# A two-layer transformer tower on one core: normalisation moved to ScalarE, one part of the maxima moved behind the values, three pieces of weights rounded later

## The reference

```
h = W.T[x] + b + pe
h = h + attn(layernorm(h))      # 8 heads of 16; per row a mean and a variance of the causal dots instead of a softmax
h = h + ffn(layernorm(h))
ffn(x): hx = layernorm(x) * ln_g + ln_b
        q, k, v = hx@Wq, hx@Wk, hx@Wv;  q, k = l2norm(q)*8*qn_g, l2norm(k)*8*kn_g      # 2 heads of 64
        y = softmax(causal(q@k.T / 8)) @ v @ Wo
        gate = softmax(y@gate_W + gate_b)                                              # 8 experts
        out = sum_e gate_e * (gelu(y@W1_e + b1_e) @ W2_e + b2_e)                       # hidden width 512
```

## Time and profile before

| | us |
|---|---|
| median of 3 runs | 852.5 (849.17 to 853.72) |
| the profiled execution's own time | 850.87 |
| span in its profile | 849.1 |
| granted TensorE clock, mean | 0.978 of full |
| PE busy | 777.6 (92%) |
| DVE busy | 710.1 (84%) |
| ACT busy | 478.3 (56%) |
| POOL busy | 341.3 (40%) |

### The profile page before, as it was taken

One profiled execution on the slowest core, in us unless ns is written; L12 is line 12 of the kernel. 1 busy time (PEld: TensorE's weight loads), 2 busy tenths in 40 slices (PEclk: granted clock), 3 DMA queues, 4 the chain that ended last, 5 costly groups with the idle time before them and its releaser, 6 DMA issues.

```text
span 849.1 us, 21002 instructions
## 1 busy us (share of the span) xinstructions
PE 777.6 (92%) x8208; PEld 555.6 (65%) x8208; DVE 710.1 (84%) x1585; ACT 478.3 (56%) x997; POOL 341.3 (40%) x386
## 2 busy tenths in 40 slices
PE   2799999999876789998889889999999999999997
PEld 1668887788644455555556556777777777777775
DVE  3668899888489776776777878999999999999997
ACT  2436555555255667776879666455555555555553
POOL 6649999777365557666667530000000000000000
PEclk9899999999799999999999999999999999999999
DMA  3101011000000000000000000000000000000000
GB/s 130 56 8 35 23 38 38 25 26 17 10 1 1 1 2 2 2 3 2 2 14 3 2 2 2 2 14 2 14 1 14 2 14 2 14 2 14 2 14 14
DMA packets 9666, 12.09 MB, mean 14 GB/s; under 512 B 1856, under 2 KB 6592, under 8 KB 9568
## 3 DMA queue, kind: packets, MB, share of 16 engines
q1 hardware_dynamic: 8544, 8.65, 3.4%
q0 software_dynamic: 1024, 2.10, 0.9%
HBM read 8.65 MB, written 2.10 MB: 13 GB/s over the span
## 4 chain that ended last, share of the span: by engine, by line
PE 75%; DVE 9%; ACT 7%; issue 5%; POOL 2%; DMA 1%; DVEq 0%; ACTq 0%; POOLq 0%
PE ps L988 73%; DVE mx L834 2%; DVE room L944 1%; ACT room L562 1%; DVE room L942 1%; ACT room L553 1%; ACT qk L492 1%; DMA h_all<-emb_rows,idx 1%; DVE mx L829 1%; PE ps L1016 1%; DVE och L911 0%; ACT qh L499 0%; PE ps L996 0%; ACT kh L501 0%; ACT hxT L481 0%
## 5 line engine op out<-in xcount | busy, mean ns | idle before, releaser
L577 ACT ACTIVATE cst<-ps,col 128x512 f32<-128x512 f32 x256 | 176.1, 689 | 164.0 <-PE ps L988 163.2
L988 PEld LDWEIGHTS ps<-arena,sq 128*128 128x128 f16 x3072 | 192.2, 98 | 62.1 <-DVE sq L972 4.2
L988 PE MATMUL ps<-arena,sq 128*128 128x128 f16 x3072 | 213.1, 219 | 0.5 <-DVE sq L972 0.5
L988 PE MATMUL ps<-y,arena 128*128 128x512 f16 x768 | 208.7, 382 | 1.3 <-DVE och L911 1.3
L972 DVE TENSOR_TENSOR sq<-cst,sq 128x512 f16<-128x512 f32 x256 | 175.8, 687 | 4.4
L373 POOL TENSOR_TENSOR room<-room 128x512 f16<-128x512 f32 (+3 forms) x122 | 123.6, 1032 | 74.2 <-ACT room L562 72.6
L967 DVE CAST sq<-cst 128x512 f16<-128x512 f32 x256 | 108.9, 425 | 11.5 <-ACT cst L577 4.2
L553 ACT ACTIVATE room<-ps 128x512 f32<-128x512 f32 (+3 forms) x160 | 76.7, 533 | 41.3 <-PE ps L988 40.9
L834 DVE TENSOR_REDUCE mx<-ps 128x2 f32<-128x1024 f32 (+2 forms) x64 | 70.1, 1096 | 30.4 <-PE ps L988 30.2
L988 PEld LDWEIGHTS ps<-y,arena 128*128 128x128 f16 x768 | 65.0, 98 | 34.0 <-issue 3.4
L960 DVE SCALAR_TENSOR_TENSOR h_all<-ps,gs,h_all 128x128 f32<-128x128 f32 x256 | 77.2, 344 | 1.0 <-PE ps L988 0.9
(11 more groups left out here) (158 smaller groups left out, 1186.9 us busy)
## 6 DMA issues: line engine op xcount, KB each, us to landing
sq<-w_rows SPq DMA_DIRECT2D x16, 256.0 KB, 2.8
out<-h_all SPq DMA_DIRECT2D x32, 64.0 KB, 1.6
cst<-consts SPq DMA_DIRECT2D x1, 896.0 KB, 5.3
h_all<-emb_rows,idx POOLq DMA_INDIRECT x32, 2.6
cst<-consts SPq DMA_DIRECT2D x1, 398.0 KB, 3.3
c<-consts SPq DMA_DIRECT2D x1, 256.0 KB, 5.1
wqkv<-w_qkv SPq DMA_DIRECT2D x1, 192.0 KB, 3.4
wsm<-w_sm SPq DMA_DIRECT2D x1, 192.0 KB, 5.1
```

The costliest lines, as they stand in the source:

```text
L577: a.activation(hid[:, f], ps[:, HBANK[f], :], ACT.Gelu_apprx_tanh, bias=col[:, K_B1 + k:K_B1 + k + 1], scale=1.0 / WS).then_inc(S["hid_rea ...
L988: return t_.matmul(o, l, r, start=start, stop=stop, skip_group_check=True)
```

## The change

Four edits. The normalisation of chunks 3 to 15 goes from VectorE to ScalarE, as scale r and bias -m*r, for which VectorE negates the mean and GpSimd multiplies. In the preparing steps, `normed_T(c+3)` goes to the start of the step on TensorE and ScalarE. The 1e-12 of the l2 norm becomes a 65th column of the squares, so that GpSimd's addition goes. In the attention steps the last (or only) pair of maxima stands at the end of TensorE's step, behind the values and the output part. Pieces 13 to 15 of the weights are staged in the buffers of x2 and hxT and rounded at steps 2, 7 and 13 of the experts.

```diff
@@ sync
-            for n in range(2, NPIECE):
+            for n in range(2, NEARLY):
                 sp.wait_ge(S["wlow_ready"], n - 1)
                 sp.dma_start(stage[n % 2], ...)
+            sp.wait_ge(S["qkv2_ps"], NT)
+            sp.wait_ge(S["x2T_ps"], NT)
+            for n in range(NEARLY, NPIECE):
+                sp.wait_ge(S["wlow_ready"], n - 1)
+                sp.dma_start(late_stage[n % 2], ...)
@@ gpsimd
             def both_norms(c):
                 pool.wait_ge(S["stats2"], c + 1)
-                g.tensor_tensor(rr[:, c, 1], rr[:, c, 0], mhalf[:, 0:B], ALU.pow).then_inc(S["rr_ready"], 1)
+                g.tensor_tensor(rr[:, c, 1], rr[:, c, 0], mhalf[:, 0:B], ALU.pow).then_inc(S["neg2"], 1)
+                pool.wait_ge(S["neg2"], c + 1)
+                g.tensor_tensor(rr[:, c, 3], rr[:, c, 1], rr[:, c, 2], ALU.mult).then_inc(S["rr_ready"], 1)
...
             def l2_factors(c):
-                g.tensor_tensor(ss[:, par, 1], ss[:, par, 0], l2_eps, ALU.add).then_inc(S["l2_link"], 1)
-                pool.wait_ge(S["l2_link"], c + 1)
-                g.tensor_tensor(ss[:, par, 2], ss[:, par, 1], mhalf[:, 0:8], ALU.pow).then_inc(S["rn_ready"], 1)
+                g.tensor_tensor(ss[:, par, 1], ss[:, par, 0], mhalf[:, 0:8], ALU.pow).then_inc(S["rn_ready"], 1)
...
+            g.memset(qk2[:, :, DS:], L2_EPS).then_inc(S["eps_set"], 1)
...
-                if s in WLATE:
-                    weights_low(NEARLY + WLATE.index(s))
+            weights_low(NEARLY)
+            weights_low(NEARLY + 1)
             low_y(LAST)
+            weights_low(NEARLY + 2)
@@ scalar
+            def normed2(c):
+                act.wait_ge(S["rr_ready"], c + 1)
+                act.wait_ge(S["x2T_ps"], c - 1)
+                for b in range(B):
+                    last = a.activation(x2[c % 2][:, b], h_all[:, 2 * c + b, :], ACT.Identity,
+                                        bias=rr[:, c, 3, b:b + 1], scale=rr[:, c, 1, b:b + 1])
+                last.then_inc(S["x2_ready"], 1)
             def step_b(c):
+                if c and c + 3 < NT:
+                    normed_T(c + 3)
                 if c + 2 < NT:
                     squares(c + 2)
                 high_qk(c)
                 if c == 4:
                     ao_out(NT - 1)
-                if c + 3 < NT:
-                    normed_T(c + 3)
+                if c == 0:
+                    normed_T(3)
+                if c + 4 < NT:
+                    normed2(c + 4)
+            normed2(3)
...
-                    if s in WLATE:
-                        weights_high(NEARLY + WLATE.index(s))
@@ scalar, experts, after the gelu
+                    if n * FT + f in WLATE:
+                        weights_high(NEARLY + WLATE.index(n * FT + f))
@@ vector
+                v.tensor_scalar(rr[:, c, 2], mv2[:, c, :, 0], -1.0, None, ALU.mult).then_inc(S["stats2"], 1)
...
-                v.tensor_reduce(ss[:, c % 2, 0], qk2[:].rearrange("p b (g e) -> p (b g) e", e=DS), AX, ALU.add
+                v.tensor_reduce(ss[:, c % 2, 0], qk2[:], AX, ALU.add
...
-                if c + 3 < NT:
-                    normed2(c + 3)
@@ tensor
             def step_b(c):
+                if c and c + 3 < NT:
+                    normed_T(c + 3)
                 if c + 2 < NT:
                     pe.wait_ge(S["qkn_ready"], c + 1)
                     project2(c + 2)
...
                 unit_T(c)
-                if c + 3 < NT:
-                    normed_T(c + 3)
+                if c == 0:
+                    normed_T(3)
...
-                for part in pairs[:1]:
+                for part in pairs[:-1]:
                     pair_scores(*part)
...
-                for part in pairs[1:]:
-                    pair_scores(*part)
                 for m in range(LAST):
                     if s - YAT[m] in PE_Y:
                         out_part(m, PE_Y.index(s - YAT[m]) + 1)
+                for part in pairs[-1:]:
+                    pair_scores(*part)
@@
-WLATE = [52, 60, 66]
+WLATE = [2, 7, 13]
```

More of the change, by code:

```diff
@@ L65, in tower @@
         qkg8 = sb("qkg8", [P, 1])
-        eps = sb("eps", [P, 10])
-        ln_eps, l2_eps = eps[:, 0:2], eps[:, 2:10]
+        ln_eps = sb("eps", [P, 2])[:]
         credit = sb("credit", [P, 16])
@@ L131, in tower @@
         mv2 = sb("mv2", [P, NT, B, 2])
-        rr = sb("rr", [P, NT, 2, B])
+        rr = sb("rr", [P, NT, 4, B])
         x2_all = sb("x2", [P, 2, B, D])
@@ L136, in tower @@
         hxT = [hxT_all[:, i] for i in range(2)]
-        qk2 = sb("qk2", [P, B, 4 * DS])
-        ss = sb("ss", [P, 2, 3, B * 4])
+        qk2 = sb("qk2", [P, B * 4, DS + 1])
+        ss = sb("ss", [P, 2, 2, B * 4])
         qkn = sb("qkn", [P, B, 4 * DS])
@@ L304, in _ @@
             g.memset(mpad[:], 0.0).then_inc(S["setup"], 1)
-            pool.wait_ge(S["setup"], 10)
+            pool.wait_ge(S["setup"], 9)
             pool.wait_ge(S["load_a"], 32)
@@ L430, in weights_high @@
                 act.wait_ge(S[STAGED[n % 2]], 16 * (n // 2 + 1))
-                a.activation(w12[:, 4 * n:4 * n + 4, 0, :], stage[n % 2].rearrange("p (w d) -> p w d", d=D),
+                raw = stage[n % 2] if n < NEARLY else late_stage[n % 2]
+                a.activation(w12[:, 4 * n:4 * n + 4, 0, :], raw.rearrange("p (w d) -> p w d", d=D),
                              ACT.Copy, scale=WS)
-                a.activation(scaled[n % 2], stage[n % 2], ACT.Copy, scale=WS).then_inc(S["whigh_ready"], 1)
+                a.activation(scaled[n % 2], raw, ACT.Copy, scale=WS).then_inc(S["whigh_ready"], 1)
             a.preload_act_table(ACT.Exp)
@@ L491, in squares @@
                     act.wait_ge(S["wlow_ready"], NEARLY - 1)
-                a.activation(qk2[:], ps[:, q:q + B, 0:2 * D], ACT.Square).then_inc(S["sqqk"], 1)
+                a.activation(qk2[:, :, 0:DS].rearrange("p (b g) e -> p b g e", b=B),
+                             ps[:, q:q + B, 0:2 * D].rearrange("p b (g e) -> p b g e", e=DS), ACT.Square
+                             ).then_inc(S["sqqk"], 1)
                 a.copy(v16[:, 2 * c:2 * c + B, :, 0:DS],
@@ L735, in stats2 @@
                 dve.wait_ge(S["agg2"], c + 1)
-                v.tensor_scalar(rr[:, c, 0], mv2[:, c, :, 1], 1.0 + LN_EPS, LN_EPS * LN_EPS, ALU.mult, ALU.add
-                                ).then_inc(S["stats2"], 1)
+                v.tensor_scalar(rr[:, c, 0], mv2[:, c, :, 1], 1.0 + LN_EPS, LN_EPS * LN_EPS, ALU.mult, ALU.add)
+                v.tensor_scalar(rr[:, c, 2], mv2[:, c, :, 0], -1.0, None, ALU.mult).then_inc(S["stats2"], 1)
             def step_a(c, nxt, more=2, first=False):
@@ L947, in _ @@
                     row_max(*two[1], (0, 1))
-            dve.wait_ge(S["wlow_ready"], NPIECE)
+            dve.wait_ge(S["wlow_ready"], NEARLY)
             def add_rows(n, r):
@@ L1059, in _ @@
                 project_rows(1, 1, b)
-            pe.wait_ge(S["setup"], 10)
+            pe.wait_ge(S["setup"], 9)
             pe.wait_ge(S["dt_sb"], B)
@@ L1124, in normed_T @@
                     pe.wait_ge(S["hxT_sb"], c)
-                if c == 7:
+                if c == 8:
                     pe.wait_ge(S["aoT_sb"], NT)
-                if c == 8:
+                if c == 9:
                     pe.wait_ge(S["h1_ready"], NT)
@@ L1186, in step_b @@
                 if c == 4:
-                    pe.wait_ge(S["hxT_sb"], 7)
+                    pe.wait_ge(S["hxT_sb"], 8)
                     out_T(NT - 1)
                 if c == 5:
-                    pe.wait_ge(S["hxT_sb"], 8)
+                    pe.wait_ge(S["hxT_sb"], 9)
                     out_project(NT - 1)
                 unit_T(c)
-                if c + 3 < NT:
-                    normed_T(c + 3)
+                if c == 0:
+                    normed_T(3)
                 if c < 5:
@@ L1400, in down @@
                     pe.wait_ge(S["eo_used"], 4 * n + 4)
+                    if NEARLY - E <= n < E:
+                        pe.wait_ge(S["wlow_ready"], E + n + 1)
                 w = E * FT + n % E * FT + f
```

14 lines of the change are left out of this document (8 added, 6 removed).

## The result

| | before | after |
|---|---|---|
| median, in one set of runs | 852.18 us (849.17 to 853.72) | 863.23 us (861.44 to 866.75) |
| ratio, 95% interval | | 1.0139 (1.0096 to 1.0182) |
| profiled execution, span | 850.87, 849.1 us | 863.94, 862.1 us |
| mean granted clock | 0.978 | 0.968 |
| start of the first attention step | 284.91 | 296.61 |

From here on a difference in us that stands beside a measured time is the ratio to the kernel before, on 852 us. A comparison of rows is of one trace with one trace.

What follows compares the result with a forecast made beforehand. It took TensorE's chain as the bound, closed in first stage and experts, with a TensorE-ScalarE loop in the preparing steps. 0.8 + 3.8 - 5.0 - 2.0 + 0.4 = -2.0 us gave 850.5 on the median's scale, range 844.5 to 857.

Steps and rivals of the forecast that it cites:

- First stage, +0.8: First attention stage: GpSimd's added multiply lengthens its loop and delays the coefficients, stalling TensorE by 0.8 us.
- 0.36 of lag: First stage: the part of GpSimd's 1.2 us lag claimed free, between L697's end and TensorE's transpose; 0.8 stalls TensorE.
- 1.7 "if 0.28 counts in full": First stage, upper bound: +1.7 us if the multiply's 0.28 us counts in full.
- Preparing steps, +3.8: Preparing steps: the TensorE-ScalarE loop grows from 3.73 to 4.26 us a step; +3.8 us in sum, from +1.5 to +5.5.
- double load of step 0: Preparing steps' start: hxT(3) and the x2 both lie in step 0; steps 1 and 2 add 0.8 and 0.5 us.
- Attention reorder, -5.0: Attention steps: late maxima no longer hold the values; -5 us, from -9.1 to +2.6.
- forecast -2.0: Whole kernel: the sum of all terms, -2.0 us against the profiled execution.
- fifteen waits: Attention steps: TensorE's waits at a lone pair of maxima, each giving at most 0.84 us, together 9.1.
- Rival (3): Attention, odd steps 19 to 61: late maximum holds VectorE's low half; reorder gives nothing or costs 2.6; 856.8 us; chance 0.22.
- Weights, -2.0 and +0.4: Weight pieces 13 to 15: attention steps 52, 60, 66 gain 2.0 us (0 to 3); experts lose 0.4 (0 to 2.6).
- rival (5): Experts: GpSimd's subtractions stop VectorE in full, +2.6 us in place of +0.4, so 852.7 us; chance 0.10.

Runs made afterwards that it cites:

- with filler: Changed kernel plus four filler products on TensorE ahead of each single maximum's scores in preparing steps 6 to 12: 859.56 us, ratio 1.0102.

## Why the prediction was wrong

- **First stage, +0.8: mis-sized.** It gave GpSimd's own loop 0.11 us of slack a step and let 0.36 of lag go free. The rows show 12.29 against 11.91, and the multiply with its hand-over delays the coefficient power by 0.38 (1.23 for 0.85), not 0.28: GpSimd's loop had no slack in these steps, and the whole 0.38 counts in about six of them. That is +2.2 with the two small operations alone, and 3.3 in the changed kernel's trace, whose 13.21 no run explains. Its bound, 1.7 "if 0.28 counts in full", was the right case and still too small.
- **Preparing steps, +3.8: the loop right, the clock missing.** Interval 4.19 for 4.26, with the normed rows' pair at 0.77 for 0.74. That it came so near is in part luck: in the chain the transposes take 0.44 where 0.26 was counted, and the products 1.31 where 1.54 was, which nearly cancel. Its terms add up to 3.7, not 3.8. At the full clock the stage lost a little less than that. The first interval of 5.01 is the double load of step 0, which was counted (it is 5.06 with filler too), and chunk 2 to chunk 4 takes 9.20 us against 7.94, +1.3 as forecast. Of the 6.2 us, 3.0 are what the three intervals of 5.01 to 5.48 at the lower clock have beyond 4.19, which leaves 3.2; the kernel with filler, which has none of them, lost 3.5. The sum took all products at the duration that they had before. A loop stretched by work on ScalarE leaves TensorE idle longer: in steps at the full clock it was busy 10.51 of 17.00 us in the kernel without the reorder (270 to 287 us), against 15.37 of 22.34 before (259.56 to 281.90). That this is why the clock fell is likely, not shown. The earlier trace rows gave a clock of 1.00, and the prediction didn't ask what held it there.
- **Attention reorder, -5.0: the failed step.** It measured +3.3, which is 8.3 of the 13.8 us between the forecast -2.0 and +11.8. "the next maximum waits for it, but so does the next pair, so that chain only shifts" followed the maximum to the next maximum alone. head_out stands in the same queue, and the next item's values wait for it. And a pair moved behind the values no longer fills their wait: the prediction counted what a late pair stops holding up, not what an early one covers. The first of its fifteen waits, at 318.12 in the earlier trace rows, is such a pair: it was booked as a gain of 0.84, and it stood in time that TensorE would have spent waiting for och. Rival (3) had the right sign and the wrong place: the low half cost 2.8 us of waits before (L944) and 3.2 after. Its end at +2.6 for the reorder was short of +3.3.
- **Weights, -2.0 and +0.4: right in sum.** -2.2 measured for both (0.6 to 3.8 by the interval), where -1.6 was forecast; by the exponentials 1.0, 0.4 and 0.2 for the forecast 1.0, 0.7 and 0.3, and nothing lost in the experts for the forecast 0.4. The hits of rival (5) came, but not its cost.
- **The whole.** The three parts measured apart sum to 8.9 + 3.3 - 2.2 = +10.0, and the change to +11.8 (8.2 to 15.5): no interaction is needed. Of the +8.9, 2.5 (GpSimd's starts) and 3.7 (project2 of chunk 1 to 15) are found in the rows of that kernel's trace, 6.2 in all. The rest shows in attention steps whose order is that of before: 2.7 us behind at step 70, 1.6 of them from step 4. It need not be the change's: the kernel reordered from step 39 on, with the code of before up to there, stood 2.9 behind at step 6 and 4.3 at step 12 of its trace. In the 28 us that begin 2 us ahead of the first exponential the granted clock is 0.82 and 0.76 in these two, and 0.94 before. So I take both for the clock; no run isolates it, and why it fell there stays open.
- The Trainium skill (Perfetto Trace Analysis, Optimizing Scalar/DVE Operations) says that with a saturated DVE, offloading some work to Scalar may make sense. Here it did not: VectorE's busy time fell by 9.92 us of 38 and the stage grew.

## What to carry to other kernels

An instruction moved later in a queue has two prices: all that stands behind its consumer on the consumer's engine, not only the next of its kind, and the waits that it used to fill where it stood. An engine that is half idle is still the wrong place for work from the busiest engine, if the half-idle one is in the chain that sets the time of a step. And what is worth a try everywhere may be worth keeping only in some steps: the same reorder costs 3.3 us in all steps and gives 4.3 outside the neighbourhood of head_out.

## What the hardware showed that I had not expected

A stall may be paid twice, but the second price is not a fixed one. At 332.30 in the changed kernel TensorE comes out of 1.84 us of waiting for och, and its 24 small products of the values take 1.49 where those of before took 0.91 after a wait of 0.67. The granted clock of the two stretches:

```profile
328.00:332.30 4.30, 1.14 (x20) 0.64 (x17) 3.72 (x5) 2.08 (x7) 3.91 (x5) 1.00 0.00 0
332.30:336.00 3.70, 3.69 (x64) 3.35 (x66) 0.88 (x4) 0.83 (x4) 1.13 (x3) 0.54 0.00 0
```

TensorE was busy 1.14 of 4.30 us before it fell. In the three traces with the reorder everywhere (the changed kernel, the one with filler and the reorder alone) the clock falls at steps 10, 18 and 26 each time; between steps 3 and 30 the trace before has one such stretch, at step 18, and the one with the reorder away from head_out has none. But the long wait is not needed for it. The kernel reordered from step 39 on has the old order at step 10 and the wait of 0.67 of the kernel before, and there the clock fell as well, after 1.91 busy us of 4.30, and the same 24 products took 1.50:

```profile
320.85 1.34 PEld L988 LDWEIGHTS ps<-v,room 128*128 128x128 f16 x24 [0.67 <-DVE och L911]
320.86 1.50 PE L988 MATMUL ps<-v,room 128*128 128x65 f16 x24 [0.50 <-DVE och L911]
320.80:324.00 3.20, 3.14 (x53) 2.80 (x54) 1.27 (x5) 0.83 (x4) 1.64 (x4) 0.51 0.00 0
```

In the preparing steps the same pause recurs in each step at 4.19 us, and the clock fell in some of them only. So a gain or loss of a few waits in this kernel comes with a share of clock that scatters by some us; executions of the kernel before lay between 848.5 and 855.6 us in one set.
